# Quantised rows turned by transposing transfers from SBUF to SBUF instead of by TensorE, PSUM and ScalarE

## The chip, the cores and the metric

The kernel runs on one core of a Trainium2 chip. The metric is device time in microseconds (us) of one execution. A core has TensorE (PE, matrix products into the eight banks of PSUM), VectorE (DVE), ScalarE (ACT), GpSimd (POOL) and SyncE (SP), each working through its own list of instructions in order. They meet only at semaphores. Transfers between HBM and SBUF, or from SBUF to SBUF, are issued by an engine's queue and carried by 16 DMA engines; in this kernel SP issues nearly all of them. Transfers and matrix inputs use SBUF, and no transfer reads PSUM.

## What is computed

One layer over 2048 rows of 256 numbers: an attention over 1601 context rows that keeps each row's 32 largest scores, and then a feed-forward part whose activations and weights are quantised.

```python
x = x + xattn(layernorm(x), ctx, top_k=32, Wq, bq, Wk, bk, Wv, bv, Wo, bo)   # softmax over the 32 largest of 1601 scores
x = x + ffn(layernorm(x), w1, b1, w2, b2)

def act_quant(x):
    scale = 127.0 / clip(max(abs(x), axis=-1), 1e-05)
    return clip(round(x * scale), -128.0, 127.0) / scale

def bitlinear(x, w, b):                       # w becomes -1, 0 or 1 times its mean absolute value
    return einsum('bsd,fd->bsf', act_quant(rmsnorm(x)), weight_quant(w)) + b

h = gelu(bitlinear(x, w1, b1))                # 256 -> 1024
return bitlinear(h, w2, b2)                   # 1024 -> 256
```

Each row is quantised twice: `y1` (256 numbers, the input of the first product) and `y2` (1024 numbers, the input of the second). A product on TensorE sums over partitions, so both must be turned: rows lie on partitions when they are quantised, and features must lie there for the product. A quantised number is an integer between -127 and 127, exact in bf16.

## The kernel before

The 2048 rows are 16 tiles of 128 rows, worked on in 8 pairs. After a part that loads and folds the weights and the context, a loop over rounds r = 0 to 8 interleaves the stages. In round r, TensorE does the attention of pair r (`turn_weights`, `weighted`), the scores of pair r+1 (`turn_queries`, `scores`), and the feed-forward part of pair r-1 (`turn_y1`, `up`, `turn_y2`, `down`). "Even" and "odd" are the tiles 2r and 2r+1; `up_even` and `up_odd` are 2r-2 and 2r-1. The order of every engine is written out by hand as a list of calls for a round, and a call that must wait holds up all calls behind it on its engine. 

Rows are rounded by adding the number MAGIC = 12582912.0 in float32, which leaves the integer in the low bits; taking MAGIC off again gives the integer. Before the change the adding is done by `quantise_1` on POOL (L694) and `quantise_2` on ACT (L888), into float32. TensorE turns the raised rows by 128 x 128 blocks into PSUM against the identity (`turn_blocks`, L243): 4 blocks for `y1` of a pair, 8 for `y2` of a tile. ACT then copies them from PSUM to SBUF as bf16 and takes MAGIC off in the same pass (`take_y1`, `take_y2`, through `take`, L760). `up` (L403) and `down` (L422) multiply them.

The four free banks of PSUM are shared: in the loop `TURN` (banks 0 and 1) holds turned blocks and `RESULT` (banks 2 and 3) the sums of `weighted`, `up` and `down`. `fill` hands them out in turn, and TensorE waits there until the bank's last contents have been read.

What stands in a row on each engine, where the change touches it (round r):

- **PE**: `turn_queries`, `turn_weights` and `weighted` of the even tile, with `turn_y1`, then `up(up_even, 0)` ahead of `weighted(even, 3)`, which is the last part of the even tile's attention; then scores and the other `up`s, the odd tile's attention, `turn_y2`, `down(up_even)`, `turn_weights(even + 2, 0)`, `down(up_odd)`.
- **DVE**: `output(up_even - 2)` (L1197, the result of the last round's `down`), `candidates` (L1064), `output(up_odd - 2)`, the search for the 32 largest of the odd tile, `count(odd)` (L1106), `weigh(odd)` (L1099, which needs ACT's exponentials, L849), `attended(even)` (L1148 and L1150, which needs `weighted(even, 3)`), `hidden` (L1177, which needs `up`); then the same search for tile even + 2, `attended(odd)`, its statistics (`moments`, L1157) and `candidates(odd + 2, 1)`.
- **SP**: the two stores of the round (L565, after the two `output`s), `turn_counts(odd)` (L559, which waits for `count(odd)`), `load_residual(even + 2)` (L554), `turn_counts(even + 2)`, `load_residual(odd + 2)` (which waits for the statistics of `attended(odd)`), and up to round 4 two loads of `x_in` (L548).
- **ACT**, at the end of a round: `quantise_2` of both tiles, `take_y2`, and copies of scores (L807).

Of the kernel before, what the change touches and what calls it, by code (L numbers as in the profile page):

```python
# [14 lines left out]
P = 128  # L15
# [37 lines left out]
def build(nc, x, ctx, Wq, bq, Wk, bk, Wv, bv, Wo, bo, w1, b1, w2, b2, out):  # L53
# [4 lines left out]
    with ExitStack() as stack:  # L58
# [12 lines left out]
        with ExitStack() as early:  # L71
            def early_sb(name, shape, dt=F32):
                return early.enter_context(nc.sbuf_tensor(name, shape, dt))

            w1_sb = early_sb("w1_sb", [P, FB, D])
            w2_sb = early_sb("w2_sb", [P, DC, F])
# [4 lines left out]
        y2 = sb("y2", [P, 2, F])  # L81
        y2T = sb("y2T", [P, FB, 2 * P], BF16)
# [5 lines left out]
        y1 = sb("y1", [P, 2, D])  # L88
        y1T = sb("y1T", [P, DC, 2 * P], BF16)
# [98 lines left out]
        g_ready, g_sq_ready, g_max_ready = sem("g_ready"), sem("g_sq_ready"), sem("g_max_ready")  # L188
        row2_step, y2_ready = sem("row2_step"), sem("y2_ready")


        place, uses, last = {}, [0] * 4, {EARLY: -1, TURN: -1, RESULT: -1}

        def fill(job, group):

            last[group] = (last[group] + 1) % len(group)
            k = group[last[group]]
# [22 lines left out]
        def live(j):  # L220
            return 0 <= j < PAIRS

# [7 lines left out]
        def _(pe):  # L230
# [24 lines left out]
            def fold_queries():  # L255
# [8 lines left out]
                full(ins, "wkq")  # L264
                bank = fill("k_bias", EARLY)
                pe.wait_ge(bqk_in, 2 * 16)
# [120 lines left out]
            def turn_y1(j):  # L387

                pe.wait_ge(y1_ready, (j + 1) * 2)
                turn_blocks(("y1", j), TURN, [(y1[:, u, c * P:(c + 1) * P], c * D + u * P)  # L390
                                              for c in range(DC) for u in range(2)])

            def up(t, h):

                if h == 0:
                    wait_drained(pe, ("y1", t // 2))
                if t == 0 and h == 0:
                    for k in range(4):
                        wait_drained(pe, ("w1", k))
                bank = fill(("up", t, h), RESULT)  # L400
                u = t % 2
                for c in range(DC):
                    ins = pe.matmul(bank[:, :], y1T[:, c, u * P:(u + 1) * P], w1T[:, c, h * BANK:(h + 1) * BANK],  # L403
# [3 lines left out]
            def turn_y2(t, h):  # L407

                pe.wait_ge(y2_ready, t + 1)
                turn_blocks(("y2", t, h), TURN, [(y2[:, t % 2, (h * 4 + k) * P:(h * 4 + k + 1) * P], k * P) for k in range(4)])  # L410

            def down(t):

                for h in range(2):
                    wait_drained(pe, ("y2", t, h))
# [5 lines left out]
                for b in range(FB):  # L421
                    ins = pe.matmul(bank[:, 0:D], y2T[:, b, u * P:(u + 1) * P], w2T[:, b, :],  # L422
# [7 lines left out]
            for k in range(5):  # L430
                turn_context(k)
# [885 lines left out]
```

## Time and profile before

| | |
|---|---|
| median of 3 runs | 314.02 us (313.54 to 315.88) |
| the profiled execution | 317.03 us, its span 315.0 us |
| mean granted TensorE clock | 0.967 |
| busy: PE, DVE, ACT, POOL | 283.6, 246.0, 208.0, 130.2 us |
| one round in the middle (143.5 to 173.9 us) | 30.4 us |

The span runs from the first to the last instruction; the time of the execution holds about 2 us around it. The durations below come from that one execution. "Idle before" is time in which an engine stood still before a group of instructions, and the name behind it is what released it. In the timeline each line begins with the start in us and the duration in us; `x2` at the end means two instructions in a row under one line.

### The profile page before, as it was taken

Reading aid. Unit: us, or ns where it says so; the run is one execution under the profiler, and the core shown is the slowest. Engines: PE = TensorE matmul, PEld = TensorE weight load, DVE = VectorE, ACT = ScalarE, POOL = GpSimd, SP = SyncE. Lnnn points to the kernel's source line nnn. Section 1 sums busy time; section 2 is a strip of 40 time slices with the busy share of each in tenths; the row PEclk is TensorE's granted clock in tenths of the full one; section 3 lists DMA queues with packets and bytes.
Section 4 is the critical chain, followed back from the end, with each engine's and each line's share of the span. In section 5 each row is a group of like instructions: output and inputs, shape, how many; then the busy total and the mean of one; then the engine's idle time right before and its main releaser. Section 6 shows DMA issues by size and latency. Waiting matters only on the chain. (4 is left out here: it accounts for less than half of the span.)

```text
span 315.0 us, 5565 instructions
## 1 busy us (share of the span) xinstructions
PE 283.6 (90%) x1640; PEld 246.8 (78%) x1640; DVE 246.0 (78%) x974; ACT 208.0 (66%) x317; POOL 130.2 (41%) x223
## 2 busy tenths in 40 slices
PE   8798997999999699999899989998999999798425
PEld 8697996899789598998698879887898888566114
DVE  2363498688999779989998999899989998963511
ACT  0554466545758874997399649855985796386452
POOL 4024601097863177127721863185316043305330
PEclk9889997999999999999999999999999999979957
DMA  7971001000100110002001100110001001000000
GB/s 182 315 280 33 3 2 32 0 16 7 50 2 17 37 50 0 3 17 86 1 1 41 61 2 17 50 37 0 19 19 33 3 17 33 20 0 1 33 0 33
DMA packets 14124, 12.23 MB, mean 39 GB/s; under 512 B 3853, under 2 KB 13646, under 8 KB 14094
## 3 DMA queue, kind: packets, MB, share of 16 engines
q1 hardware_dynamic: 13278, 11.09, 11.4%
q0 software_dynamic: 272, 0.79, 0.9%
q8 instruction: 13, 0.21, 0.3%
q14 instruction: 17, 0.14, 0.2%
q10 hardware_dynamic: 544, 0.00, 0.1%
HBM read 9.77 MB, written 2.10 MB: 38 GB/s over the span
## 5 line engine op out<-in xcount | busy, mean ns | idle before, releaser
L382 PE MATMUL bank<-vo,pT 128*128 128x257 f32 (+1 forms) x416 | 101.7, 386 | 2.2 <-ACT pT L857 1.9
L382 PEld LDWEIGHTS bank<-vo,pT 128*128 128x128 f32 (+1 forms) x416 | 75.9, 193 | 14.6 <-ACT pT L857 3.8
L1064 DVE MAX8 cand<-s_sb 128x8 f32<-128x50 f32 (+1 forms) x512 | 61.9, 196 | 8.1 <-ACT s_sb L807 5.2
L807 ACT ACTIVATE s_sb<-score 128x400 f32<-128x400 f32 x64 | 31.5, 507 | 36.1 <-PE score L235 36.0
L235 PE MATMUL score<-k_high,q_low 128*128 128x400 f32 (+1 forms) x128 | 51.1, 399 | 0.0
L235 PE MATMUL score<-k_low,q_high 128*128 128x400 f32 (+1 forms) x128 | 44.2, 345 | 0.0
L235 PE MATMUL score<-k_high,q_high 128*128 128x400 f32 (+1 forms) x128 | 44.1, 344 | 0.0
L857 ACT ACTIVATE pT<-bank 128x512 f32<-128x512 f32 x64 | 32.1, 515 | 16.0 <-PE bank L243 16.0
L243 PE MATMUL bank<-ident,e_all 128*128 128x128 f32 (+1 forms) x208 | 33.4, 283 | 1.3 <-ACT pT L857 0.7
L243 PE MATMUL bank<-ident,y 128*128 128x128 f32 x160 | 23.5, 289 | 11.3 <-ACT y L888 9.8
L1099 DVE SCALAR_TENSOR_TENSOR e_all<-s_sb,best,e_all 128x1601 f32<-128x1601 f32 x16 | 30.8, 1922 | 2.7 <-ACT e_all L849 2.7
L243 PEld LDWEIGHTS bank<-ident,y 128*128 128x128 f32 x160 | 19.8, 149 | 14.9 <-ACT y L888 11.9
L243 PEld LDWEIGHTS bank<-ident,e_all 128*128 128x128 f32 (+1 forms) x208 | 26.1, 145 | 6.6 <-DVEq L1138 2.1
L720 POOL TENSOR_SCALAR row<-g_ssq 128x2 f32<-128x2 f32 x8 | 1.5, 191 | 71.3 <-ACT g_sq L879 54.9
L629 POOL TENSOR_SCALAR xn<-x_in,ln_mv,ln_r 128x256 f32<-128x256 f32 x16 | 27.5, 1720 | 0.9
L849 ACT ACTIVATE e_all<-s_sb,neg_max 128x1601 f32<-128x1601 f32 x16 | 26.1, 1629 | 0.7 <-DVE neg_max L1077 0.6
L1177 DVE SCALAR_TENSOR_TENSOR g<-bank,row,b_bc 128x512 f32<-128x512 f32 x32 | 23.5, 741 | 3.1 <-PE bank L403 2.6
L235 PEld LDWEIGHTS score<-k_high,q_low 128*128 128x128 f32 x128 | 24.2, 189 | 1.9
L403 PE MATMUL bank<-w1T,y1T 128*128 128x512 bf16 x64 | 19.2, 385 | 6.7 <-DVE x L1150 4.9
L235 PEld LDWEIGHTS score<-k_low,q_high 128*128 128x128 f32 x128 | 24.2, 189 | 0.8
L235 PEld LDWEIGHTS score<-k_high,q_high 128*128 128x128 f32 x128 | 24.1, 188 | 0.0
L1074 DVE MAX8 best<-cand_left 128x8 f32<-128x256 f32 x48 | 20.6, 428 | 1.7
(132 smaller groups left out, 514.0 us busy)
## 6 DMA issues: line engine op xcount, KB each, us to landing
x_in<-in_x SPq DMA_DIRECT2D x16, 128.0 KB, 2.3
w_sb<-in_L_ffn_w SPq DMA_DIRECT2D x2, 1024.0 KB, 11.9
x_res<-in_x SPq DMA_DIRECT2D x16, 128.0 KB, 2.1
out<-o_sb SPq DMA_DIRECT2D x16, 128.0 KB, 1.7
ctx_sb<-in_ctx SPq DMA_DIRECT2D x3, 512.0 KB, 10.1
b_bc<-in_L_ffn_b POOLq DMA_DIRECT2D x1, 512.0 KB, 8.2
w_q<-in_L_xattn_Wq SPq DMA_DIRECT2D x1, 256.0 KB, 3.3
w_k<-in_L_xattn_Wk SPq DMA_DIRECT2D x1, 256.0 KB, 4.7
```

The source lines that it names most:

```text
L235: ins = pe.matmul(out, a, b, start=(i == 0), stop=(i == len(steps) - 1))
L243: ins = pe.transpose(bank[0:src.shape[1], at:at + rows], src, ident[0:rows, 0:rows])
L382: ins = pe.matmul(bank[:, 0:DV], pT[0:n, t % 2, b * P:(b + 1) * P], vo[0:n, b, :], start=(b == 0), stop=(b == SB - 1))
L403: ins = pe.matmul(bank[:, :], y1T[:, c, u * P:(u + 1) * P], w1T[:, c, h * BANK:(h + 1) * BANK], start=(c == 0), stop=(c == DC - 1))
L629: pool.tensor_scalar(xn[:, u, :], x_in[:, u, :], ln1_mv[:, u, 0:1], ln1_r[:, 1, u:u + 1], ALU.subtract, ALU.mult).then_inc(xn_ready, 1)
L807: act.activation(s_sb[:, t % 2, at:at + n], score[c][:, 0:n], ACT.Copy).then_inc(s_copied, 1)
L849: act.activation(e_all[:, t % 2, :], s_sb[:, t % 2, :], ACT.Exp, bias=neg_max[:, t % 2:t % 2 + 1], scale=SCALE).then_inc(e_ready, 1)
L857: drain(act.activation(pT[0:rows, t % 2, lo * P:hi * P], bank(("p", t, q))[0:rows, 0:(hi - lo) * P], ACT.Copy), ("p", t, q))
L1064: ins = dve.max(cand[:, t % 2, 8 * k:8 * k + 8], s_sb[:, t % 2, k * PIECE:end])
L1074: dve.max(best[:, u, k, :], cand_left[:, u, :] if k else cand[:, u, :]).then_inc(topk_step[u], 1)
L1099: dve.scalar_tensor_tensor(e_all[:, u, :], s_sb[:, u, :], least_kept(t), e_all[:, u, :], ALU.is_ge, ALU.mult).then_inc(masked, 1)
L1177: drain(dve.scalar_tensor_tensor(g[:, u, h * BANK:(h + 1) * BANK], src[:, :], row1[:, j % 2, 6, u:u + 1], b1_bc[:, h * BANK:(h + 1) * BANK ...
```

## The change

The rows are quantised in two passes. The first adds MAGIC as before, into a new tile `y1_raised` or `y2_raised`; the second takes MAGIC off and writes bf16 into `y1` (on POOL) or `y2` (on ACT, `lower_2`). SP then issues a transposing transfer from SBUF to SBUF, `dma_start_transpose`, straight into `y1T` (one for a pair, 128 x 512 bf16) or `y2T` (one for a tile, 128 x 1024 bf16). `turn_y1`, `turn_y2` leave TensorE, and `take_y1`, `take_y2` leave ACT. `up` and `down` wait for the transfers. `y1T` and `y2T` are laid out by tile. Beside this, `fill` now takes the bank of the group that was used longest ago, the bias of the keys is folded in a function of its own at the same place, the pass of `normalise` is split in two functions called one behind the other, and two early tiles swap their places in SBUF.

```diff
-        y2 = sb("y2", [P, 2, F])
-        y2T = sb("y2T", [P, FB, 2 * P], BF16)
+        y2_raised = sb("y2_raised", [P, 2, F])
+        y2 = sb("y2", [P, 2, F], BF16)
+        y2T = sb("y2T", [P, 2, FB, P], BF16)
...
-        y1 = sb("y1", [P, 2, D])
-        y1T = sb("y1T", [P, DC, 2 * P], BF16)
+        y1_raised = sb("y1_raised", [P, 2, D])
+        y1 = sb("y1", [P, 2, D], BF16)
+        y1T = sb("y1T", [P, 2, DC, P], BF16)
...
-            k = group[last[group]]
+            k = min(group, key=lambda b: latest[b])
+            latest[k] = len(place)
...
-            def turn_y1(j):
-
-                pe.wait_ge(y1_ready, (j + 1) * 2)
-                turn_blocks(("y1", j), TURN, [(y1[:, u, c * P:(c + 1) * P], c * D + u * P)
-                                              for c in range(DC) for u in range(2)])
-
             def up(t, h):
 
-                if h == 0:
-                    wait_drained(pe, ("y1", t // 2))
-                if t == 0 and h == 0:
+                pe.wait_ge(y1_turned, (t // 2 + 1) * 16)
...
-            def turn_y2(t, h):
-
-                pe.wait_ge(y2_ready, t + 1)
-                turn_blocks(("y2", t, h), TURN, [(y2[:, t % 2, (h * 4 + k) * P:(h * 4 + k + 1) * P], k * P) for k in range(4)])
-
             def down(t):
 
-                for h in range(2):
-                    wait_drained(pe, ("y2", t, h))
+                pe.wait_ge(y2_turned[t % 2], (t // 2 + 1) * 16)
...
-                if late:
-                    turn_y1(r - 1)
...
-                    turn_y2(up_even, 0)
-                    turn_y2(up_even, 1)
                 if more:
                     scores(odd + 2, 3)
                 if late:
-                    turn_y2(up_odd, 0)
-                    turn_y2(up_odd, 1)
                     down(up_even)
...
+            def turn_y1(j):
+
+                sp.wait_ge(y1_ready, 2 * j + 2)
+                if j:
+                    for h in range(2):
+                        wait_full(sp, ("up", 2 * j - 1, h))
+                sp.dma_start_transpose(y1T[:, :, :, :].rearrange("p u c n -> p (u c) n"),
+                                       y1[:, :, :].rearrange("p u d -> p (u d)")).then_inc(y1_turned, 16)
+
+            def turn_y2(t):
+
+                sp.wait_ge(y2_lowered, t + 1)
+                if t >= 2:
+                    wait_full(sp, ("out", t - 2))
+                sp.dma_start_transpose(y2T[:, t % 2, :, :], y2[:, t % 2, :]).then_inc(y2_turned[t % 2], 16)
...
                     turn_counts(2 * r + 1)
+                if live(r - 1):
+                    turn_y1(r - 1)
                 if live(r + 1):
                     load_residual(2 * r + 2)
                     turn_counts(2 * r + 2)
                     load_residual(2 * r + 3)
                 if live(r + 3):
                     load_x(r + 3)
+                if live(r - 1):
+                    turn_y2(2 * r - 2)
+                    turn_y2(2 * r - 1)
...
+            def quantise_1(j, u):
+
+                t = 2 * j + u
                 if j:
-                    wait_full(pool, ("y1", j - 1))
-                for u in range(2):
-                    t = 2 * j + u
-                    pool.tensor_scalar(y1[:, u, :], cen[:, t % 4, :], row1[:, j % 2, 5, u:u + 1], MAGIC,
-                                       ALU.mult, ALU.add).then_inc(y1_ready, 1)
+                    pool.wait_ge(y1_turned, j * 16)
+                if t >= 2:
+                    pool.wait_ge(y1_ready, t - 1)
+                pool.tensor_scalar(y1_raised[:, u, :], cen[:, t % 4, :], row1[:, j % 2, 5, u:u + 1], MAGIC,
+                                   ALU.mult, ALU.add).then_inc(y1_raised_ready, 1)
+                pool.wait_ge(y1_raised_ready, t + 1)
+                pool.tensor_scalar(y1[:, u, :], y1_raised[:, u, :], MAGIC, None, ALU.subtract).then_inc(y1_ready, 1)
...
-            def take_y1(j):
-
-                if j:
-                    wait_full(act, ("up", 2 * j - 1, 1))
-                take(("y1", j), y1T[:, :, :], two_parts(("y1", j)), bias=unmagic_col[:, 0:1])
...
-                    wait_full(act, ("y2", t - 2, 1))
-                act.activation(y2[:, t % 2, :], g[:, t % 2, :], ACT.Identity, scale=row2[:, j % 2, 5, t % 2:t % 2 + 1],
+                    act.wait_ge(y2_lowered, t - 1)
+                act.activation(y2_raised[:, t % 2, :], g[:, t % 2, :], ACT.Identity, scale=row2[:, j % 2, 5, t % 2:t % 2 + 1],
                                bias=magic_col[:, 0:1]).then_inc(y2_ready, 1)
 
-            def take_y2(t, h):
-
+            def lower_2(t):
+
+                u = t % 2
+                act.wait_ge(y2_ready, t + 1)
                 if t >= 2:
-                    wait_full(act, ("out", t - 2))
-                u = t % 2
-                take(("y2", t, h), y2T[:, h * 4:h * 4 + 4, u * P:(u + 1) * P],
-                     bank(("y2", t, h))[:, :].rearrange("p (b n) -> p b n", b=4), bias=unmagic_col[:, 0:1])
+                    act.wait_ge(y2_turned[u], t // 2 * 16)
+                act.activation(y2[:, u, :], y2_raised[:, u, :], ACT.Identity, bias=unmagic_col[:, 0:1]).then_inc(y2_lowered, 1)
...
-                    take_y2(up_even, 0)
-                    take_y2(up_even, 1)
+                    lower_2(up_even)
+                    lower_2(up_odd)
                 if more:
                     copy_scores(odd + 2, 1)
                     copy_scores(odd + 2, 2)
-                if late:
-                    take_y2(up_odd, 0)
```

On SP, from the end of round 3 into round 4 (`counts_row` is `turn_counts`, `x_res` is `load_residual`), there stood:

```order
L554 DMA x_res<-in_x 128x256
L548 DMA x_in<-in_x 128x256 x2
L565 DMA out<-o_sb 128x256 x2
L559 DMA counts_row<-counts 1x128x1
L554 DMA x_res<-in_x 128x256
```

and now stands:

```order
L550 DMA x_res<-in_x 128x256
L544 DMA x_in<-in_x 128x256 x2
L572 DMA_TRANSPOSE y2T<-y 128x8x128 x2
L577 DMA out<-o_sb 128x256 x2
L555 DMA counts_row<-counts 1x128x1
L564 DMA_TRANSPOSE y1T<-y 128x4x128
L550 DMA x_res<-in_x 128x256
```

Both transfers of `y2` stand behind the loads that end the round, and the one of `y1` stands behind the stores and behind the first `turn_counts` of the next.

On PE, from the end of a round into the next up to the last part of the even tile's attention (`ident,y` are the blocks of `y1` and `y2`, `ident,e_all` those of the attention weights), there stood:

```order
L243 MATMUL bank<-ident,y 128x128 x8
L422 MATMUL bank<-w2T,y2T 128x256 x8
L243 MATMUL bank<-ident,e_all 128x128 x4
L422 MATMUL bank<-w2T,y2T 128x256 x8
L243 MATMUL bank<-ident,xn 128x128 x4
L243 MATMUL bank<-ident,e_all 128x128 x4
L382 MATMUL bank<-vo,pT 128x257 x4
L243 MATMUL bank<-ident,e_all 128x128 x4
L243 MATMUL bank<-ident,e_all 65x128
L382 MATMUL bank<-vo,pT 128x257 x4
L243 MATMUL bank<-ident,y 128x128 x4
L382 MATMUL bank<-vo,pT 128x257 x4
L403 MATMUL bank<-w1T,y1T 128x512 x2
L382 MATMUL bank<-vo,pT 128x257
```

and now stands:

```order
L420 MATMUL bank<-w2T,y2T 128x256 x8
L250 MATMUL bank<-ident,e_all 128x128 x4
L420 MATMUL bank<-w2T,y2T 128x256 x8
L250 MATMUL bank<-ident,xn 128x128 x4
L250 MATMUL bank<-ident,e_all 128x128 x4
L393 MATMUL bank<-vo,pT 128x257 x4
L250 MATMUL bank<-ident,e_all 128x128 x4
L250 MATMUL bank<-ident,e_all 65x128
L393 MATMUL bank<-vo,pT 128x257 x8
L407 MATMUL bank<-w1T,y1T 128x512 x2
L393 MATMUL bank<-vo,pT 128x257
```

The blocks of `y1` and `y2` are gone, nothing else has moved, and the first product of `y1` (L407) still stands ahead of the last product of the even tile's attention (L393, one matmul).

## Rows read from the trace of the kernel before

**Rows 1.** The page, busy time, share and instructions of each engine

```profile
PE 283.6 (90%) x1640; PEld 246.8 (78%) x1640; DVE 246.0 (78%) x974; ACT 208.0 (66%) x317; POOL 130.2 (41%) x223
```

**Rows 2.** Windows, one middle round: length, busy PE, PEld, DVE, ACT, POOL, clock, DMA

```profile
143.50:173.90 30.40, 29.54 (x176) 25.75 (x174) 28.64 (x120) 23.30 (x35) 15.07 (x26) 1.00 0.09 28
```

**Rows 3.** Groups of instructions: busy us, mean ns of one, idle before

```profile
L243 PE MATMUL bank<-ident,y 128*128 128x128 f32 x160 | 23.5, 289 | 11.3 <-ACT y L888 9.8 <-POOL y L694 0.8 <-ACT y2T L760 0.7
...
L760 ACT ACTIVATE y2T<-bank,unmagic_col 128x512 bf16<-128x512 f32 x32 | 20.6, 685 | 1.9 <-PE bank L243 1.1
...
L888 ACT ACTIVATE y<-g,magic_col,row 128x1024 f32<-128x1024 f32 x16 | 18.9, 1232 | 4.3 <-POOL row L725 4.3
```

**Rows 4.** Timeline, end of round 3 into round 4

```profile
166.71 2.37 ACT L888 ACTIVATE y<-g,magic_col,row 128x1024 f32<-128x1024 f32 x2
...
171.77 0.91 SPq L548 DMA_DIRECT2D x_in<-in_x  x2
...
172.81 1.04 PE L422 MATMUL bank<-w2T,y2T 128*128 128x256 bf16 x8
...
173.99 0.47 DVE L1197 SCALAR_TENSOR_TENSOR o_sb<-bank,row,x2b 128x256 f32<-128x256 f32 x1
```

**Rows 5.** Timeline, round 4 up to the even tile's attention

```profile
176.45 0.93 POOL L694 TENSOR_SCALAR y<-cen,row 128x256 f32<-128x256 f32 x2
...
177.70 1.63 ACT L849 ACTIVATE e_all<-s_sb,neg_max 128x1601 f32<-128x1601 f32 x1
...
180.88 0.59 PE L403 MATMUL bank<-w1T,y1T 128*128 128x512 bf16 x2
...
181.31 0.60 PE L382 MATMUL bank<-vo,pT 65*128 65x257 f32 x2
...
181.52 0.48 SPq L559 DMA_DIRECT2D counts_row<-counts  x1
...
183.21 0.16 DVE L1148 RECIPROCAL inv_sum<-bank 128x1 f32<-128x1 f32 x1
```

**Rows 6.** DMA issues: KB each, median us from issue to landing

```profile
x_in<-in_x SPq DMA_DIRECT2D x16, 128.0 KB, 2.3
...
out<-o_sb SPq DMA_DIRECT2D x16, 128.0 KB, 1.7
...
w_q<-in_L_xattn_Wq SPq DMA_DIRECT2D x1, 256.0 KB, 3.3
...
w_o<-in_L_xattn_Wo SPq DMA_DIRECT2D x1, 256.0 KB, 10.0
```

**Rows 7.** DMA queue of SP: packets, MB, share of 16 engines

```profile
q1 hardware_dynamic: 13278, 11.09, 11.4%
```

**Rows 8.** Timeline, end of round 1 into round 2

```profile
108.46 0.91 SPq L548 DMA_DIRECT2D x_in<-in_x  x2
...
112.87 0.48 DVE L1197 SCALAR_TENSOR_TENSOR o_sb<-bank,row,x2b 128x256 f32<-128x256 f32 x1 [0.43 <-PE bank L422]
```

**Rows 9.** Timeline, the last two pairs of tiles

```profile
285.78 2.37 ACT L888 ACTIVATE y<-g,magic_col,row 128x1024 f32<-128x1024 f32 x2 [1.38 <-POOL row L725]
...
292.13 0.48 DVE L1197 SCALAR_TENSOR_TENSOR o_sb<-bank,row,x2b 128x256 f32<-128x256 f32 x1 [0.56 <-PE bank L422]
...
294.29 1.04 PE L403 MATMUL bank<-w1T,y1T 128*128 128x512 bf16 x4 [0.84 <-ACT y1T L760]
...
303.80 2.37 ACT L888 ACTIVATE y<-g,magic_col,row 128x1024 f32<-128x1024 f32 x2 [2.90 <-POOL row L725]
...
308.87 2.93 PE L422 MATMUL bank<-w2T,y2T 128*128 128x256 bf16 x16
...
310.92 0.48 DVE L1197 SCALAR_TENSOR_TENSOR o_sb<-bank,row,x2b 128x256 f32<-128x256 f32 x1 [9.95 <-PE bank L422]
311.94 0.48 DVE L1197 SCALAR_TENSOR_TENSOR o_sb<-bank,row,x2b 128x256 f32<-128x256 f32 x1 [0.54 <-PE bank L422]
```

**Rows 10.** Windows, after TensorE had stood idle; the columns of rows 2

```profile
302.00:304.00 2.00, 0.00 (x0) 0.00 (x0) 0.00 (x0) 0.20 (x1) 1.56 (x6) 0.50 0.00 0
```

More of the change, by code:

```diff
@@ L221, in live, with later @@
             return 0 <= j < PAIRS
+        def later(j):
+            return 0 < j < PAIRS
         def ctx_blocks(c):
@@ L421, in down, with warm @@
                 for b in range(FB):
-                    ins = pe.matmul(bank[:, 0:D], y2T[:, b, u * P:(u + 1) * P], w2T[:, b, :],
+                    ins = pe.matmul(bank[:, 0:D], y2T[:, u, b, :], w2T[:, b, :],
                                     start=(b == 0), stop=(b == FB - 1))
                 full(ins, ("out", t))
-            pe.wait_ge(ident_ready, 2)
-            for _ in range(WARM):
-                pe.transpose(score[0][:, 0:P], ident[:, :], ident[:, :])
+            def warm():
+                pe.wait_ge(ident_ready, 2)
+                for _ in range(WARM):
+                    pe.transpose(score[0][:, 0:P], ident[:, :], ident[:, :])
+            warm()
             fold_queries()
+            fold_key_bias()
             for k in range(5):
@@ L726, in row_scales_2 @@
                 pool.tensor_scalar(dq, step_size, wmean[:, 1:2], None, ALU.mult).then_inc(row2_step, 1)
-            normalise(0)
+            normalise_scale(0)
+            for u in range(2):
+                normalise(0, u)
             spread_value_bias()
             split_queries(0)
-            normalise(1)
+            normalise_scale(1)
+            for u in range(2):
+                normalise(1, u)
             join_biases()
@@ L737, in _ @@
                     row_scales_1(r - 1)
-                    quantise_1(r - 1)
+                    for u in range(2):
+                        quantise_1(r - 1, u)
                 if live(r):
@@ L747, in _ @@
                 if live(r + 2):
-                    normalise(r + 2)
+                    normalise_scale(r + 2)
+                    for u in range(2):
+                        normalise(r + 2, u)
                 if live(r - 1):
@@ L903, in _ @@
             take_folded_queries()
+            take_key_bias()
             for k in range(5):
@@ L951, in _ @@
                     sum_weights(1, w2_sb)
-                if late:
-                    take_y1(r - 1)
                 if more:
```

27 lines of the change are left out of this document (14 added, 13 removed).

## Prediction, on record before the changed kernel was timed

> **What bounds the kernel now.** I read the page's busy times first: TensorE is busy for 90% of the span, VectorE for 78% [rows 1]. That average hides the loop, so I cut one round out of the timeline, from `output` to `output`. Of 30.4 us TensorE is busy 29.5 and VectorE 28.6 [rows 2]: both are full, and whoever loses a microsecond loses it for the kernel. A busy TensorE is not TensorE at its peak, but VectorE's share is a share of real work: taking work from TensorE alone can bring a round down to no less than 28.6 us, and 30.4 - 28.6 = 1.8 us is the most that a round can give. In the other direction nothing protects it: a wait put in front of VectorE lengthens the round by nearly all of itself. So the timeline around the two places where VectorE depends on the turned rows decides, and SP's queue with it.
>
> **What is removed.** 160 blocks, 23.5 us of TensorE [rows 3], 2.9 us a round. On ACT 32 copies of 0.69 us for `y2T` [rows 3] go, 2.7 us a round, and one more of that kind for `y1T`. Since new waits open on TensorE (below), I count nothing for the blocks in the loop: the time saved is spent waiting for what they delivered.
>
> **What is added on ACT and POOL.** `lower_2` is one more pass over 128x1024 for each tile; `quantise_2` is the same shape, two of them in 2.37 us, so 1.19 each [rows 4]. ACT gives 2.4 us a round for the 2.7 it is spared, and it has 7 us of slack [rows 2]: nothing. The order does matter: both tiles are raised, then both lowered, so the even tile is ready 3 x 1.19 = 3.6 us after the start, at 166.71 + 3.57 = 170.3, the odd one at 171.5. POOL lowers `y1` in two more passes of about 0.47 us [rows 5]; `y1` is then ready at about 176.45 + 1.9 = 178.3. Both are hidden behind SP, which gets there later.
>
> **The price of a transposing transfer.** The trace has none, nor any transfer from SBUF to SBUF of this size. Nearest by bytes: the one for `y1` moves 128 KB, as `x_in` does (2.3 us to landing) and `out` (1.7); the one for `y2` 256 KB, as the first weight load, 3.3 us [rows 6]. I take 2.3 and 3.3. Low end: 1.7 for both, the fastest landing of a full tile. High end: if the turned data travels in 256-byte pieces, `y2` is 1024 of them. A packet of SP's queue costs 11.4% x 16 x 315 / 13278 = 43 ns [rows 7]; 64 on each of 16 engines is 2.8 us, and beside a base of 1.7 that is 4.5 us; 3.1 for `y1`. The second transfer of `y2` I let land 1.5 us after the first, between one issue (0.46, half of the pair of `x_in`) and a whole 3.3. The Trainium skill ("Advanced Engine Details and Errata", X-Bar Transpose (TRN2)) says that transposing DMAs on this chip are as fast as plain ones. By that rule my values stand; no row here shows it.
>
> **First place, the start of a round.** VectorE begins round 4 with `output` of tile 4 at 173.99 [rows 4]. SP issues the transfer of tile 4's `y2` only behind the loads that end round 3. Those wait for VectorE's own `attended(odd)`, and end at 171.77 + 0.91 = 172.68 [rows 4]. So landing is at 172.68 + 3.3 = 175.98. Then come the eight matmuls of `down` and `output`. At full clock that is 1.18 us (172.81 to 173.99 [rows 4]). But TensorE has then had nothing to do since its scores; their matmuls would end near 170, with the blocks gone, so for some 6 us. In the tail, where it has no work before the last blocks, the granted clock stood at 0.50 by 302 [rows 10], the lower of its two levels (1.2 and 2.4 GHz), and there the same step took 308.87 to 310.92 = 2.05 us [rows 9]. I take 2.05: `output` at 178.0, **4.0 us late**. This holds in rounds 3 to 5. In rounds 6 and 7 no `x_in` loads stand in the way (0.91 less): 3.1. In round 2: 108.46 + 0.91 + 3.3 + 2.05 = 114.7 against 112.87 [rows 8], 1.9. Sum: 1.9 + 3 x 4.0 + 2 x 3.1 = 20.1 us.
>
> **Second place, the middle of a round.** `turn_counts(odd)` waits for VectorE's count; SP is through with it at 181.52 + 0.48 = 182.0 [rows 5], and only then issues the transfer of `y1`. It lands at 184.3. TensorE stands at `up(up_even, 0)`, with the last product of the even tile's attention queued behind. Before, the pair of groups took 180.88 to 181.91 [rows 5], 1.0 us; so `attended(even)` can start at 185.4 instead of 183.21 [rows 5]: **2.2 us late**, in each of rounds 1 to 7, 15.4 us. `weigh` hides 1.9 us of the chain already; this is what sticks out.
>
> Between the two, TensorE restarts late: the odd tile's transfer lands at 177.5, its `down` (slow clock) ends near 180.8 instead of 173.85, and the exponentials, at 177.70 [rows 5] before, end near 186.3, about 1 us after VectorE wants them at 185.4. That delay lies ahead of the second wait and is swallowed by it. Nothing.
>
> **The tail.** Pair 6: raising starts at 285.78 [rows 9], the even tile is lowered at 289.35 and lands at 292.65, the odd one at 294.15; the two `down`s bring the second `output` to about 296.3 against 292.13 [rows 9]. On SP the transfer of the last `y1` stands behind that store: 296.8 + 0.35 + 2.3 = 299.5, against an `up` at 294.29 [rows 9]: 5.2 us, and 0.5 for `up` at the low clock. Pair 7: raising 303.80 + 5.7 = 309.5, three passes 313.1, second landing 317.9, last `output` at 319.9 against 311.94 [rows 9]: 8.0 us. Here the blocks' savings are in the sum.
>
> **Sum**: 20.1 + 15.4 + 8.0 = 43.5 us. The profiled execution took 317.03 us, 3.0 more than the median of the runs, 314.02. So 360.5 on its own footing, and **357.5 on the median's**.
>
> **Low end** (1.7 us each, clock kept): second place 1.6 x 7 = 11.2; first place 172.68 + 1.7 + 1.18 = 175.6, so 1.6 in three rounds, 0.7 in two, 0 in round 2: 6.2; tail 2. That is 19 us: 333. **High end** (4.5 and 3.1, second landing 2.8 after the first): second place 3.0 x 7 = 21; first 5.2 x 3 + 4.3 x 2 + 3.1 = 27.3; tail 14. That is 62: 376; 378 with rounding.
>
> **Rivals.**
>
> *The blocks go through the crossbar one after another.* Then the price follows the blocks, not the bytes. For it: `y2` has eight blocks of 128x128, and two-byte elements are the smallest this kernel moves in bulk. Against it: nothing in the rows. The longest landing of 256 KB in the trace is 10.0 us (`w_o`, behind other loads [rows 6]). With 10 for `y2`, 5 for `y1`, and the second `y2` another 10 behind, the round waits 10.7 at the first `output`, some 7 at the second and 5 at the attention: 23 us. Six rounds, 5 us in round 1, and a tail of 35 make 178: about 490 us. The Trainium skill ("VectorE: DVE Perf Modes", The three transpose paths) gives 1309 ns for one 128x128 block by the crossbar. If eight followed each other at that, `y2` would take 10.5 us; if most of it is a fixed cost, it speaks for my values. Half of this case may be milder, 380 to 430. Chance of anything above the range 10%.
>
> *Short transfers, and TensorE was the bound: faster.* If a transfer within SBUF landed in under 1 us, having no trip to HBM, the waits would be about 0.9 at the second place and 1.3 at the first, at full clock. Should TensorE's relief of 2.9 us a round [rows 3] shorten the same path, the round would gain 0.7 us, and the tail about 3, since its blocks ran at the low clock: 314 - 5 - 3 = 306. It decides from the point where both waits together fall under 2.9 us. Against it: even the 128 KB store lands in 1.7 us [rows 6], the waits are VectorE's and not TensorE's, and VectorE leaves only 1.8 us a round [rows 2]. Chance 3%; no change to be told, 1%.
>
> *A milder slowing*, 317 to 333: landings under 1.7 us, but still on VectorE's path. 5%. *The clock is not lost*: 0.9 less in six rounds, about 351, within the range. That the change does not do what it says is excluded by SP's order, which shows the transfers.
>
> **Numbers.** 357 us, with 81% for 333 to 378, which the low and high ends set. A difference of 1% is what a measurement of this kernel can tell from none. Faster 3%, same 1%, slower 96%.
>
> **What would show it.** SP's issue of the two `y2` transfers directly behind `x_in`, near the start of each round, and landing after 3.3 us; idle time of VectorE before `output` released by TensorE's `down`, about 4 us a round, and before `attended` about 2.2; TensorE at 0.5 of its clock for some microseconds in each round, where rounds now show 1.00; rounds of 36 to 37 us instead of 30.4. If VectorE's idle time is small and rounds are near 30, I mis-sized the landing; if `output` waits but `attended` does not, the SP order at the second place is not what I think; if the landing follows the number of blocks, the first rival holds.

## The result, and the profile after

The changed kernel takes **366.66 us** (median of 4 runs, 365.6 to 368.23) against 313.8 us for the kernel before on the same chip (313.54 to 315.88): a ratio of 1.167, 95% interval 1.161 to 1.174. It is 52.9 us slower. I had said 357 us and 333 to 378: the side and the range held, and the middle was 9.7 us short. The profiled execution took 366.79 us, its span 364.9 against 315.0 before, so 49.9 us of span have to be found.

The page after, busy time of each engine and SP's queue:

```profile
PE 278.0 (76%) x1472; PEld 235.9 (65%) x1480; DVE 249.8 (68%) x974; ACT 199.2 (55%) x293; POOL 143.7 (39%) x239
...
q1 hardware_dynamic: 34526, 16.34, 17.4%
```

VectorE does the same 974 instructions as in [rows 1], in 3.8 us more; its share falls from 78% to 68%, so nearly all of the new time is time in which it stands. TensorE has 168 matmul records less (the 160 blocks, and 8 of `up` that the record lacks) and is busy only 5.6 us less, since what is left of its work runs partly at the lower clock. The queue has 21,248 packets more than [rows 7] for 5.25 MB more, 247 bytes each.

The waits of the changed kernel (total us, times, longest us):

```profile
DVE o_sb L1217 <- PE bank L420: 42.2, 10, 11.6
...
DVE inv_sum L1168 <- PE bank L393: 14.4, 8, 3.1
DVE g L1197 <- PE bank L407: 7.9, 7, 4.2
...
DVE e_all L1119 <- ACT e_all L880: 5.2, 5, 1.5
```

The same four waits before:

```profile
DVE o_sb L1197 <- PE bank L422: 14.1, 5, 9.9
...
DVE e_all L1099 <- ACT e_all L849: 2.7, 2, 1.8
...
DVE g L1177 <- PE bank L403: 2.6, 2, 2.4
DVE inv_sum L1148 <- PE bank L382: 2.3, 1, 2.3
```

`output` (`o_sb`) and `attended` (`inv_sum`) are the first and the second place of the prediction. Together the four grow by 48.0 us; the span grew by 49.9. Of the 21.7 us before, 18.6 lie in the tail, which begins with the attention of the last even tile.

The first place, at the start of round 4 (timeline: start, us, and in brackets the idle time before and its releaser). It answers to [rows 4]:

```profile
180.77 2.36 ACT L913 ACTIVATE y_raised<-g,magic_col,row 128x1024 f32<-128x1024 f32 x2
...
183.04 2.17 ACT L922 ACTIVATE y<-y_raised,unmagic_col 128x1024 bf16<-128x1024 f32 x2
...
185.37 0.34 SPq L550 DMA_DIRECT2D x_res<-in_x  x1
...
185.75 0.91 SPq L544 DMA_DIRECT2D x_in<-in_x  x2
...
186.76 2.67 SPq L572 DMA_TRANSPOSE y2T<-y  x2
...
190.26 1.89 PE L420 MATMUL bank<-w2T,y2T 128*128 128x256 bf16 x8 [6.45 <-DMA y2T<-y]
...
192.29 0.48 DVE L1217 SCALAR_TENSOR_TENSOR o_sb<-bank,row,x2b 128x256 f32<-128x256 f32 x1 [4.24 <-PE bank L420]
```

Read it upwards from the last line. VectorE stood 4.24 us for `down` (4.0 were forecast). TensorE had stood 6.45 us for the transfer ("some 6"). The first transfer was issued at 186.76, directly behind the two `x_in` loads, and landed 3.5 us later. The even rows had been ready since about 184.1, half-way through ACT's second group: 2.6 us of the wait are made by the queue's order and not by the transfer.

The second place, in the middle of round 4; it answers to [rows 5]:

```profile
199.84 0.49 SPq L555 DMA_DIRECT2D counts_row<-counts  x1
200.43 1.21 SPq L564 DMA_TRANSPOSE y1T<-y  x1
...
203.20 0.58 PE L407 MATMUL bank<-w1T,y1T 128*128 128x512 bf16 x1 [2.61 <-DMA y1T<-y]
...
203.57 1.06 PE L393 MATMUL bank<-vo,pT 65*128 65x257 f32 x2
204.67 0.17 DVE L1168 RECIPROCAL inv_sum<-bank 128x1 f32<-128x1 f32 x1 [3.06 <-PE bank L393]
...
207.29 0.75 DVE L1197 SCALAR_TENSOR_TENSOR g<-bank,row,b_bc 128x512 f32<-128x512 f32 x1 [1.09 <-PE bank L407]
```

The rows of `y1` were ready at 193.3, and their transfer was issued at 200.43, when `turn_counts` was through. `attended` waited 3.06 us in this round; over the seven rounds the wait is 12.1 us. The last line is one I had not foreseen: TensorE comes late to the other products too, and `hidden` waits another 1.09.

The granted clock behind either wait (columns of [rows 2]; the clock is the number before the last two):

```profile
190.20:192.30 2.10, 2.04 (x10) 1.60 (x11) 0.01 (x1) 0.00 (x0) 1.92 (x4) 0.50 0.23 43
203.20:206.00 2.80, 2.80 (x8) 2.53 (x8) 1.29 (x4) 0.00 (x0) 0.20 (x1) 0.51 0.00 0
```

It is the lower level at both places. The prediction had it at the first only. At the second, it took 1.7 us from the landing (200.43 + 2.5 = 202.9) to `attended` at 204.67, where 1.1 was put in, and 2.5 to the landing where 2.3 was: so 3.1 and not 2.2 in this round.

Four rounds in a row, from `output` to `output`, with the same columns:

```profile
154.90:192.29 37.39, 29.99 (x155) 25.61 (x155) 29.09 (x118) 22.23 (x32) 16.20 (x27) 0.87 0.17 39
192.29:231.53 39.24, 30.01 (x155) 25.55 (x155) 28.88 (x118) 22.22 (x32) 16.61 (x28) 0.89 0.17 38
231.53:268.11 36.58, 29.23 (x155) 24.88 (x155) 29.20 (x119) 22.22 (x32) 15.93 (x27) 0.92 0.15 34
268.11:304.08 35.97, 29.68 (x155) 25.36 (x155) 28.22 (x114) 22.22 (x32) 11.97 (x24) 0.88 0.15 34
```

A round lasts 36 to 39 us instead of 30.4 (36 to 37 were forecast), the clock is at 0.87 to 0.92 instead of 1.00, and no engine is full: TensorE and VectorE each stand 6 to 10 us a round.

The end of the tail, where [rows 9] had 303.80 to 311.94:

```profile
351.68 2.37 ACT L913 ACTIVATE y_raised<-g,magic_col,row 128x1024 f32<-128x1024 f32 x2 [2.93 <-POOL row L747]
353.96 2.17 ACT L922 ACTIVATE y<-y_raised,unmagic_col 128x1024 bf16<-128x1024 f32 x2
355.12 2.61 SPq L572 DMA_TRANSPOSE y2T<-y  x2
358.42 3.12 PEld L420 LDWEIGHTS bank<-w2T,y2T 128*128 128x128 bf16 x16 [13.87 <-DMA y2T<-y]
...
362.15 0.48 DVE L1217 SCALAR_TENSOR_TENSOR o_sb<-bank,row,x2b 128x256 f32<-128x256 f32 x1 [1.22 <-PE bank L420]
```

From raising to the last `output` it is 10.5 us instead of 8.1: 3.4 us of passes for the even tile, 3.3 of landing, 3.7 of two `down`s at the low clock.

### The profile page after: what moved, and what is told of

Same layout as the page of the kernel before. It is cut to its first block and busy times, and to the rows that moved or that the text cites. A ratio compares the mean times of both kernels' runs of the same rounds, so it can differ in the third digit from the quotient of the medians.

```text
span 364.9 us, 5253 instructions
## 1 busy us (share of the span) xinstructions
PE 278.0 (76%) x1472; PEld 235.9 (65%) x1480; DVE 249.8 (68%) x974; ACT 199.2 (55%) x293; POOL 143.7 (39%) x239
## 3 DMA queue, kind: packets, MB, share of 16 engines
q1 hardware_dynamic: 34526, 16.34, 17.4%
## 5 line engine op out<-in xcount | busy, mean ns | idle before, releaser
L393 PE MATMUL bank<-vo,pT 128*128 128x257 f32 (+1 forms) x416 | 100.1, 384 | 2.4 <-ACT pT L888 2.4
L393 PEld LDWEIGHTS bank<-vo,pT 128*128 128x128 f32 (+1 forms) x416 | 75.9, 191 | 14.6 <-ACT pT L888 4.4
L420 PE MATMUL bank<-w2T,y2T 128*128 128x256 bf16 x128 | 28.9, 406 | 55.3 <-DMA y2T<-y 55.3
L888 ACT ACTIVATE pT<-bank 128x512 f32<-128x512 f32 x64 | 32.2, 516 | 50.0 <-PE bank L250 50.0
L420 PEld LDWEIGHTS bank<-w2T,y2T 128*128 128x128 bf16 x128 | 17.4, 142 | 65.0 <-DMA y2T<-y 58.5
L838 ACT ACTIVATE s_sb<-score 128x400 f32<-128x400 f32 x64 | 30.6, 502 | 48.1 <-PE score L242 48.0
L242 PE MATMUL score<-k_low,q_high 128*128 128x400 f32 (+1 forms) x128 | 44.9, 351 | 0.0
L250 PE MATMUL bank<-ident,e_all 128*128 128x128 f32 (+1 forms) x208 | 35.6, 297 | 1.7 <-ACT pT L888 1.4
L1217 DVE SCALAR_TENSOR_TENSOR o_sb<-bank,row,x2b 128x256 f32<-128x256 f32 x16 | 7.7, 484 | 42.6 <-PE bank L420 42.2
L1119 DVE SCALAR_TENSOR_TENSOR e_all<-s_sb,best,e_all 128x1601 f32<-128x1601 f32 x16 | 32.2, 2014 | 5.2 <-ACT e_all L880 5.2
L407 PE MATMUL bank<-w1T,y1T 128*128 128x512 bf16 x56 | 20.4, 450 | 18.8 <-DMA y1T<-y 17.6
L250 PEld LDWEIGHTS bank<-ident,e_all 128*128 128x128 f32 (+1 forms) x208 | 28.8, 156 | 6.9 <-issue 2.3
L895 ACT ACTIVATE g<-g 128x1024 f32<-128x1024 f32 x16 | 17.0, 1060 | 12.4 <-DVE g L1197 12.3
## 6 DMA issues: line engine op xcount, KB each, us to landing
w_sb<-in_L_ffn_w SPq DMA_DIRECT2D x2, 1024.0 KB, 11.9
```

The source lines that it names most:

```text
L242: ins = pe.matmul(out, a, b, start=(i == 0), stop=(i == len(steps) - 1))
L250: ins = pe.transpose(bank[0:src.shape[1], at:at + rows], src, ident[0:rows, 0:rows])
L393: ins = pe.matmul(bank[:, 0:DV], pT[0:n, t % 2, b * P:(b + 1) * P], vo[0:n, b, :], start=(b == 0), stop=(b == SB - 1))
L407: ins = pe.matmul(bank[:, :], y1T[:, u, c, :], w1T[:, c, h * BANK:(h + 1) * BANK], start=(c == 0), stop=(c == DC - 1))
L420: ins = pe.matmul(bank[:, 0:D], y2T[:, u, b, :], w2T[:, b, :], start=(b == 0), stop=(b == FB - 1))
L838: act.activation(s_sb[:, t % 2, at:at + n], score[c][:, 0:n], ACT.Copy).then_inc(s_copied, 1)
```

## The experiments

Three theories. **A**: the time is made by the two waits, each by the transfer's place in SP's queue, its landing, and the low clock behind the wait. **B**: the transfers slow the other engines while they run. **C**: the second passes on POOL and ACT cost it. Each kernel was timed beside the kernel before, on the same chip, and the ratios are to that; its median was 316 to 317 us in these runs.

**e1_y2_early and e2_y1_early: one transfer moved forward each.** In e1, on SP, at the end of a round:

```
+ if live(r - 1):
+     turn_y2(2 * r - 2); turn_y2(2 * r - 1)
  if live(r + 1):
      load_residual(2 * r + 3)
  if live(r + 3):
      load_x(r + 3)
- if live(r - 1):
-     turn_y2(2 * r - 2); turn_y2(2 * r - 1)
```

> The changed kernel with one edit on SP: the two transfers of y2 stand ahead of the residual load of the odd tile and of the x_in loads, not behind them. Theory A (the cost is two waits of VectorE, made by where the transfers stand on SP and by 3.3 us to landing): SP can issue the first as soon as it is lowered, 2.6 us earlier (1.7 in the rounds without x_in loads), VectorE's wait before output falls from 4.2 to about 1.6, and the kernel takes 366.7 - 14 = 353 us. Theory B (transposing transfers slow the other engines' access to SBUF, the queue's order is nothing): 365 to 368 us. Theory C (the added passes on ACT and POOL cost the time): 365 to 368 us.

In e2, on SP, in the middle of a round:

```
+ if live(r - 1):
+     turn_y1(r - 1)
  if live(r):
      turn_counts(2 * r + 1)
- if live(r - 1):
-     turn_y1(r - 1)
```

> The changed kernel with one edit on SP: the transfer of y1 stands ahead of turn_counts of the odd tile, not behind it. Theory A: it is issued when POOL is done with y1, some 7 us earlier, and lands before TensorE wants it; VectorE's wait of 3.1 us before attended goes in all seven rounds, 22 us: 345 us. Theory B and theory C: 365 to 368 us.

Measured: e1 359.05 us (355.63 to 361.54), ratio 1.130 (1.117 to 1.143); e2 353.93 us, ratio 1.120 (1.111 to 1.129). The waits of e1:

```profile
DVE o_sb L1218 <- PE bank L420: 25.7, 9, 11.6
...
DVE inv_sum L1169 <- PE bank L393: 18.3, 8, 3.3
...
DVE g L1198 <- PE bank L407: 9.6, 7, 3.8
```

and of e2:

```profile
DVE o_sb L1217 <- PE bank L420: 42.3, 10, 11.6
...
DVE inv_sum L1168 <- PE bank L393: 3.4, 7, 2.2
```

The wait that each was to take away went: before `output` 42.2 to 25.7 in e1, of which 20.2 lie in the tail as before, and before `attended` 14.4 to 3.4 in e2, where `output`'s stayed at 42.3. So in the loop both waits are made by the queue's order. (The waits of e1 are those of an execution of 361.5 us, the longest of its three.) Both gained less than expected. e2's span fell by 11.9 us, which is the 11.0 of `attended` and little else; I had taken the 3.1 us of one round for all seven, 22 us, where the seven made 12.1. e1 gained 7.6 us where its wait fell by 16.5: `attended` waits 3.9 us more and `hidden` 1.7, and VectorE's own work is 2.3 us longer (252.1 against 249.8). VectorE comes earlier to the second place, while `y1` lands when it did, in relation to `turn_counts`. So the time that the first wait gives back is partly taken by the second.

**e3_both_early: both moved.**

> Both edits of SP's order together. Theory A: the two waits are at different places of the round and add up, 14 + 22 = 36 us: 331 us, with about 1.6 us of wait before output left in each round. If the two waits hide one another, 340 to 345 us. Theory B and theory C: 365 to 368 us.

341.16 us (339.16 to 342.79), ratio 1.078 (1.068 to 1.088). The ratios of e1 and e2 lie 3.7 and 4.7 points below that of the change; both together give 8.9, no less than the sum. It is ten microseconds over the expectation, which was built on the same 14 and 22 us. Rounds are 31.4 to 33.7 us; from round 3 on up to 1.1 is left before `output`, and up to 1.2 before the use of the exponentials.

**e4_spare: the kernel before, with 24 transposing transfers that nobody waits for.** Each has the size and the queue's place of one in the changed kernel, out of a tile that is never written again.

```
+ def spare_y2(t):
+     sp.wait_ge(y2_ready, t + 1)
+     ...
+     sp.dma_start_transpose(spare2[:, t % 2, :, :], still[:, :]).then_inc(spare_in[t % 2], 16)
```

> The kernel before, with 24 transposing transfers of the same sizes at the same places of SP's queue, from a tile that never changes into tiles that nobody reads; nobody waits for them. Theory A: their data costs nobody anything; SP's loads behind them start 1 to 2.7 us later, with slack: 313 to 316 us. Theory B: most of the 53 us comes back, at least 10: over 324 us.

316.4 us, ratio 0.9996 (0.994 to 1.005), with its transfers in the page:

```profile
spare<-still SPq DMA_TRANSPOSE x24, 3.2
```

B is refuted. The same transfers at the same places cost nothing, within half a percent, when nothing depends on them. The Trainium skill ("SBUF — State Buffer", SBUF: two separate sides) says that engines and transfers use separate ports and can't slow each other; this run agrees.

**e5_filler: TensorE kept busy in the waits,** with transposes into a bank that the next product overwrites.

```
+ bank = fill(("out", t), RESULT)
+ if t % 2 == 0 and live(t // 2 + 1):
+     for _ in range(36):
+         pe.transpose(bank[:, 0:P], ident[:, :], ident[:, :])
  pe.wait_ge(y2_turned[t % 2], (t // 2 + 1) * 16)
```

> The changed kernel, in rounds 1 to 7, with 36 transposes of the identity (5.3 us at full clock) on TensorE ahead of its wait for the first y2T and 14 (2.1 us) ahead of its wait for y1T, written into the bank that the next product overwrites. They do nothing but keep TensorE busy while it would stand still. Theory A (part of the cost is the granted clock, which falls in the wait): rounds show 1.00 instead of 0.87 to 0.92; the first down takes 1.04 us, not 1.9, and VectorE's waits for up go; about 0.9 us in six and 1.2 us in seven rounds, 13 us less: 353 us. Rival (the lower clock is covered by the waits and costs nothing): 365 to 368 us, or more where the transposes overrun.

361.96 us (360.61 to 361.97), ratio 1.147 (1.137 to 1.156), between the 353 us of theory A and the 365 to 368 of the rival; the mean clock rose from 0.881 to 0.957.

```profile
DVE o_sb L1223 <- PE bank L426: 35.8, 10, 11.6
...
DVE inv_sum L1174 <- PE bank L393: 17.6, 8, 2.5
```

`output` waits 3.3 to 3.4 us in rounds 3 to 5 instead of 4.1 to 4.3: the 0.87 of the slow `down`, as put in the sum. But 3.2 us came back before `attended`, while the wait for the exponentials in front of it fell from 5.2 to 1.7: the transfer of `y1` is issued behind VectorE's own count, so VectorE meets it there whatever it gained before. The useless blocks are not what held the gain back: in the trace TensorE still stood 1.4 to 2.9 us for the first `y2T` after them, and 0.6 to 2.2 for `y1T` in six of seven rounds (in round 3 the trace shows no such wait). So the clock is worth about 5 of 53 us (2.1 points), with the transfers where they are.

**e7_y1_by_pe: only `y2` by transfer,** `y1` turned by TensorE and taken by ACT as before the change.

> The changed kernel with y1 turned as before the change (POOL writes it raised in float32, TensorE turns it, ACT lowers it out of PSUM); only y2 goes by transposing transfers. Theory A: all of the second place is undone, as in the run with the transfer of y1 put early (353.9 us), and the tail loses the landing of the last y1 too, 3 us: 351 us. If the transfer of y1 were harmless when it is early, the two would be equal; if y1 is the greater part of the damage, under 335 us.

351.52 us (350.59 to 351.59), ratio 1.114 (1.105 to 1.123), as expected. `output` still waits 41.5 us in all, `attended` 5.6. The change to `y2` alone makes 11.4 of the 16.7 points, the one to `y1` 5.3, and moving `y1`'s transfer (e2) gives nearly as much as not having it.

**e6_fitted: the waits taken away by order.** e3, and on ACT the even tile raised and lowered before the odd one, and on TensorE `up` behind the attention:

```
- quantise_2(up_even)
- quantise_2(up_odd)
- lower_2(up_even)
- lower_2(up_odd)
+ quantise_2(up_even)
+ lower_2(up_even)
+ quantise_2(up_odd)
+ lower_2(up_odd)
...
- if late:
-     up(up_even, 0)
  if now:
      weighted(even, 3)
+ if late:
+     up(up_even, 0)
```

> Both edits of SP's order (341.2 us), and two more: ACT raises and lowers the even tile before it raises the odd one, and TensorE does weighted(even, 3) ahead of up(up_even, 0). Theory A: the first landing comes 1.2 us earlier and takes the 1.1 us that VectorE still waits before output, in six rounds; the exponentials come earlier with TensorE's restart, up to 1 us: 341 - 10 = 331 us. A tail of about 9 us more than before stays. If the rest is VectorE's own time and not waits, 339 to 342 us.

332.5 us (331.26 to 334.82), ratio 1.057 (1.047 to 1.067), as expected. One of its rounds:

```profile
146.19:177.46 31.27, 27.45 (x154) 23.53 (x154) 29.48 (x120) 22.51 (x33) 16.75 (x28) 1.00 0.20 47
```

TensorE is relieved of 2.1 us against [rows 2] at full clock, and VectorE waits for neither product in it. The round is still 0.9 us longer than before, because VectorE's own work takes 29.48 us instead of 28.64. The timeline shows one reason:

```profile
152.84 1.27 POOL L655 TENSOR_TENSOR q_low<-q_full,q_high 128x512 fp32r<-128x512 f32 x1
153.13 1.26 DVE L1127 SCALAR_TENSOR_TENSOR cand_ge<-cand,best,cand_worth 128x256 bf16<-128x256 f32 x1
...
154.32 1.88 DVE L1120 SCALAR_TENSOR_TENSOR e_all<-s_sb,best,e_all 128x1601 f32<-128x1601 f32 x1
154.56 2.22 POOL L642 TENSOR_TENSOR ln_r<-ln_r,minus_half 128x2 f32<-128x2 f32 x1
```

`cand_ge` takes 1.26 us here and 0.48 where POOL is still; `ln_r`, two numbers a row, takes 2.22 where its like takes 0.7, and ends 0.6 us behind `e_all`. POOL's second passes have moved its list so that these lie side by side.

**e8_down_later: e6 with `down(up_odd)` moved into the next round.**

> As the fitted one, and TensorE does down of the odd tile one step later, behind turn_queries and turn_weights(even, 1) of the next round, which fill the time between the two landings. Theory A: VectorE's wait for the exponentials (3.2 us in all with both edits) goes: 329 us, 2 us under the fitted one. Rival: TensorE is not late there any more, and nothing changes: within 1 us of the fitted one.

332.12 us (331.06 to 333.88), ratio 1.055 (1.045 to 1.065): the same as e6, as its rival said and not theory A. TensorE's order there is worth nothing that these runs can tell.

**e9_few_blocks: the kernel before with only one block turned** of each four. This leaves TensorE's relief alone, with no transfer and no pass; ACT's copies stay. What it computes is wrong.

> The kernel before, with TensorE turning one block of every four of y1 and y2 (40 of 160); three quarters of both turned tiles are left as they were in PSUM, so the feed-forward part computes on wrong numbers. Nothing is put in the blocks' place: this is the gain that the change could have had from TensorE alone. Theory A (VectorE bounds the round): 15 blocks of 0.147 us a round, 2.2 us, are taken off TensorE and the round stays within 0.4 us of 30.4; only the head and the tail, where the blocks stand in the open at the low clock, give 2 to 3 us: 310 to 313 us. Rival (TensorE bounds it): up to 1.8 us in seven rounds more: 298 to 301 us.

316.98 us, ratio 0.999 (0.994 to 1.004), against 310 to 313 expected: a miss. One round:

```profile
143.54:173.99 30.45, 28.28 (x161) 24.19 (x161) 28.69 (x119) 23.10 (x36) 15.13 (x25) 1.00 0.10 28
```

Busy TensorE fell to 28.3 us and the round stayed at 30.4, as theory A had it. So the time that the change takes off TensorE was worth nothing to begin with, at least for the three quarters that e9 takes off; what ACT's copies cost, e9 does not test. The prediction had allowed for up to 1.8 us a round, and I had expected 2 to 3 us from head and tail: in the profile the tail is 0.8 us shorter (36.9 against 37.7, from `attended` of the last even tile to the last `output`), and the median shows nothing.

**e10_spare_passes: the kernel before with the second passes added**, into tiles that nobody reads, all else kept.

> The kernel before, with the second passes alone: POOL and ACT also write every quantised tile in bf16 into tiles that nobody reads; TensorE still turns the raised rows. Theory A: POOL's pass is hidden; ACT's two passes (2.3 us a round) stand in front of take_y2 and of two copies of scores, which have up to 1 us of slack, so at most 1 us a round comes out: 314 to 322 us. Theory C (the passes are the cost): over 335 us.

326.64 us (326.53 to 326.77), ratio 1.030 (1.026 to 1.035), over A's 314 to 322. The passes are not free: its groups show where.

```profile
L906 ACT ACTIVATE low<-y,unmagic_col 128x1024 bf16<-128x1024 f32 x16 | 17.4, 1137 | 0.0
L702 POOL TENSOR_SCALAR low<-y 128x256 bf16<-128x256 f32 x16 | 13.7, 854 | 1.4
L1125 DVE SCALAR_TENSOR_TENSOR cand_ge<-cand,best,cand_worth 128x256 bf16<-128x256 f32 x16 | 11.4, 710 | 0.6
```

POOL's pass is 0.85 us, not 0.47, `cand_ge` has a mean of 710 ns against 538 before, three middle rounds are 31.2 to 31.4 us, and the tail, where ACT's passes lie in the chain ahead of the copies from PSUM, is 4.1 us longer (41.8 against 37.7). Theory A had the rounds within its 1 us and nothing for the tail.

**e11_one_pool and e12_one_each: e6 without the second passes.** The first pass writes bf16 itself, so the rounding to whole numbers is left out. In e11 POOL's:

```
- pool.tensor_scalar(y1_raised[...], cen[...], row1[...], MAGIC, ALU.mult, ALU.add)
- pool.tensor_scalar(y1[...], y1_raised[...], MAGIC, None, ALU.subtract)
+ pool.tensor_scalar(y1[...], cen[...], row1[...], 0.0, ALU.mult, ALU.add)
```

> The kernel with both of SP's transfers moved forward, ACT's passes tile by tile and up behind weighted(even, 3) took 332.5 us, 18.7 above before, with no wait left in the loop: head +2.4, five rounds +4.7, tail +7.6, the rest between. Here POOL writes y1 in bf16 in its first pass, without the rounding to whole numbers and without the second pass, so y1's values differ a little. Theory A, what is left comes from the passes' place and length: POOL has 2.5 us a round less, q_low no longer lies beside cand_ge, which falls back from 1.2 to 0.5 us in every round; rounds 30.5 to 31, in all 322 to 327. Theory B, what is left is the transfers' own latency in the tail and head, and POOL's pass is hidden: 330 to 333.

In e12 ACT's too: `quantise_2` writes `y2` without MAGIC, and `lower_2` is gone.

> As the kernel with one pass on POOL, and ACT too writes y2 in bf16 in its first pass (rounding to whole numbers left out of y1 and y2, the second passes gone). Both transfers stay. Theory A: the tail loses the 1.2 to 2.4 us of lowering that lie in its chain for each of the last two pairs, and ACT has 2.3 us a round less: 317 to 321, 3 to 7 above before, which would be the price of the transfers themselves when they are put well. Theory B, the transfers' latency is what is left: 325 or more. Were it below 312, transfers without the second passes would beat turning by TensorE.

e11 took 330.6 us (327.63 to 333.99), ratio 1.044 (1.036 to 1.053): over theory A's 322 to 327, and its interval overlaps that of e6, 1.047 to 1.067, so POOL's pass alone isn't told apart. In its profile, that of its longest execution, `q_low` no longer lies beside `cand_ge`, which takes 0.48 us in the three middle rounds again, and VectorE's work is 247.4 us against 251.1 in e6. But its waits for the exponentials grew from 2.0 to 6.9 us: what the pass had cost came back as a wait. Why the exponentials come later there stays open. e12 took 324.23 us (323.04 to 325.28), ratio 1.028 (1.020 to 1.036), between the two theories. A round of e12:

```profile
144.96:175.90 30.94, 27.56 (x155) 23.58 (x155) 28.88 (x119) 20.06 (x30) 14.48 (x26) 1.00 0.20 47
```

VectorE is nearly back, at 28.88 us. Five rounds last 155.4 us against 152.5 before, and from there to the last `output` it is 50.4 against 46.6. I put the rest down to the transfer itself, well placed: the last two pairs have nothing to hide its 3.3 us behind. No run takes that rest apart.

By the ratios, the 16.7 points are: 8.9 for the transfers' places in SP's queue (e3), 2.1 for the orders on ACT and TensorE (e6), 2.9 for the second passes (e12), and 2.8 that even transfers without these passes cost. Each ratio has an interval of half a point to a point on either side, so the 2.1 and the 2.9 are the least sure. The small changes that came along (`fill`'s choice of banks, `normalise` in two functions, the places of two early tiles) were never run alone; whatever they cost or give is in the last 2.8.

## Why the prediction held, and where it was short

- **What bounds the kernel: right, and stronger than said.** VectorE's share was to protect nothing and any wait before it to count in full; the four waits make 48.0 of the 49.9 us. That the blocks' removal could give a round at most 1.8 us holds, and it gave none in e9.
- **The price of a transfer: right.** 3.1 to 3.6 us for `y2`, median 3.3, and 2.5 for `y1` where I took 2.3. The high end's reckoning, 43 ns for each of the 256-byte pieces, was twice too dear: the queue's share went from 11.4% of 315 us to 17.4% of 364.9, (63.5 - 35.9) x 16 / 21,248 packets = 21 ns each. The second transfer of a pair, let land 1.5 us after the first, lands 1.1 us after it in the tail. The landing that the rule of the Trainium skill ("Advanced Engine Details and Errata", X-Bar Transpose (TRN2)) gave is the one measured. The rival with the blocks in a row is out. The other rival, short transfers, had 1.3 us of wait at the first place; by its own rows it is 172.68 + 1.0 + 1.18 - 173.99 = 0.9. Nothing measured hangs on it.
- **The first place: right.** Waits before `output` of 2.96, then 4.28, 4.24, 4.07, then 3.14, 3.28: 22.0 us against 1.9 + 3 x 4.0 + 2 x 3.1 = 20.1, where 0.43 had been there before. That `x_in` costs 0.9 in rounds up to 5 shows as the step from 4.1 to 3.1.
- **The second place: right in mechanism and near in sum, by some luck.** `attended` waited 0.8 to 3.1 us, 12.1 in all, not 2.2 each time; 4.3 us more lie in front of it at `e_all`, in four rounds. Together they are 16.4 against 15.4, and 2.0 to 3.1 in each round. That the late exponentials are "swallowed" by the second wait is thus what happened: the two share one delay. The low clock behind this wait too (0.51) was missing in the sum; in round 4 it made about 0.6 us, and with the clock kept (e5) `attended` waited 2.44 there instead of 3.06.
- **The clock: right in size where it was counted.** At the first place the step from transfer to `output`, 1.18 us before, took 2.03 (190.26 to 192.29), against 2.05 put in; e5 took 0.7 to 1.0 off each round's first wait.
- **The tail: 8.9 us against 8.0.** From `attended` of the last even tile (274.21 before, 315.49 after) to the last `output` it is 37.7 us before and 46.7 after.
- **The term that was mis-sized is the loop.** Up to that `attended` the kernel lost 41.3 us and not 20.1 + 15.4 = 35.5. Idle time explains 1.4 more at `output`, 1.0 at the second place, 2.3 at `hidden` and 0.9 at the first `candidates`, places where TensorE's lateness comes through and for which my sum had nothing. And VectorE's own work up to there grew from 229.6 to 233.0 us, 3.4 more, which I had not thought of at all. Of that, 2.1 us are longer `e_all` and `cand_ge` (30.8 to 32.2 and 8.6 to 9.3 us): ACT's and POOL's slack was counted as "nothing", and a pass that is hidden on POOL can still lengthen VectorE's work beside it. That is 9.0. Some 3 us come back, mostly ahead of the loop: the first `attended` starts at 56.97 us after and at 60.62 before, so that from there on the loop lost 44.9 us. Of the 9.7 us between 357 and the median, these two terms (5.8 and 0.9) make the larger part. The other 3 are the footing: the profiled execution before stood 3 us above its median, and the one after stood at it.
- **POOL's "two more passes of about 0.47 us"** failed: the pass takes 0.85 (854 ns in the groups above).

Nothing tried beats the kernel before.

## What to carry to other kernels

Before work is moved off a busy engine, leave it out and time the kernel: where a round stays as long, as in e9, moving it has nothing to gain. A transfer in place of on-chip work adds a wait that begins when its queue gets to it; write down what stands ahead of it there, and issue it where its data is ready, which was worth more than half of the loss here. A pass on an idle engine is not free because that engine has room: look at what its neighbours will then do at the same time.

## What the runs showed of the hardware

- A transposing transfer from SBUF to SBUF holds SP's queue for 1.2 to 1.4 us, where the issue of a plain one takes 0.34 to 0.49, and lands after 3.3 us (256 KB) and 2.5 us (128 KB). Of two in a row the second lands 1.1 us behind the first in the tail (issued at 355.12 and 356.4, landed after 3.3 and 3.1 us); the two `output`s there are 1.7 us apart, with `down` at the low clock between them.
- VectorE and POOL hold each other up: in e6 `cand_ge` takes 1.26 us beside `q_low` where it takes 0.48 alone, and `ln_r` 2.22 us beside `e_all` where it takes 0.7. The Trainium skill ("SBUF — State Buffer", SBUF: two separate sides) says that a VectorE instruction with two inputs in SBUF and a GpSimd one that reads SBUF share a pair of ports, and that the later one stands until the first is through. The second case fits to 0.1 us: 156.20, the end of `e_all`, and 0.7 are 156.9, and `ln_r` ended at 156.78. The first fits but for 0.2 us: `q_low` ended at 154.11, and `cand_ge` 0.28 us later, where its own length is 0.48. The same 0.28 us behind POOL's end stands in e6 at 184.47, 216.05 and 246.62, and `e_all` at 72.55 and 85.80 ends 1.68 to 1.69 us behind POOL's `w_sb` and `q_low`, its own length being 1.88. So both stand for POOL with all but the first 0.2 us of their work. Not every overlap does this: beside POOL's `xn` at 122.27 `cand_ge` took its 0.48 us, though `xn` had started 0.6 us before it and ended 0.1 us after. e11 takes away POOL's second pass alone: `q_low` ends before `cand_ge` starts in its middle rounds, `cand_ge` takes 0.48 us there and `ln_r` 0.71.
- POOL's pass from float32 into bf16 took 0.85 us as one subtraction (`low<-y`) and 0.48 us as a multiplication and an addition (e11, `y<-cen,row`), both 128x256. So the bf16 output alone doesn't make it; what does, no run tells.
